# Whole casts in three PSUM slots, a four-tile output projection, border strips, two-step sums and new engine orders in a fused attention and convolution kernel

## The chip, the cores and the metric

The kernel runs on one core of a Trainium2 chip. The metric is the device time of one execution in microseconds (us); lower is better. Before the change the median of three runs is 110.3 us.

## What is computed

The input x holds 8 images of 16 x 16 tokens with 64 channels, all fp32. Four layers follow one another:

```python
# L0: self-attention over the 256 tokens of an image, 8-wide queries and keys, residual
out = softmax(relu(x@wq+bq) @ relu(x@wk+bk).T) @ (x@wv+bv) + x
# L1: group norm over pairs of channels, self-attention with 64-wide q and k, residual
h = group_norm(x); x = x + nin(softmax(q@k.T / 8) @ v, Wo, bo)
# L2: "hex" attention: each token attends to itself and 6 neighbours, 8 heads of 8
scores = einsum(qh, kh) / sqrt(8)            # 7 scores for each token and head
ctx    = einsum(softmax(scores), vh)         # neighbours outside the image: zero vectors
x = layernorm(x + ctx@out_w.T + out_b)
x = layernorm(x + relu(x@w1.T+b1)@w2.T+b2)
# L3: 1x1 conv (64 -> 128), grouped 3x3 conv, 1x1 conv (128 -> 64), with batch norms
out = relu(conv3(relu(bn(conv2(relu(bn(conv1(x))))))) + x)
```

## The kernel before

**Layout.** Channels lie on partitions. Two images make a pair (partitions 0 to 63 and 64 to 127), so there are PAIRS = 4 tiles of 128 x 256; two pairs make a group of 512 columns (GROUPS = 2). Each engine has its own instruction stream, written out by hand as a list of calls at the end of its block (`scalar`, `vector`, `tensor`, `gpsimd`), and semaphores tie them together. The four streams run in order, so the lists of calls set what stands behind a waiting instruction. PSUM has 8 banks of 512 fp32 columns, assigned by hand.

**Attention stage (L0 and L1).** There are 16 softmaxes n (8 images, two layers). For each: `scores` (TensorE, L933), `maxes` (VectorE, L663), `exps` (ScalarE, L438), `normalise` (VectorE, L668 and L672), `transposes` (TensorE, L944), `copy_probT` (ScalarE, L445). For each pair: `attend` (TensorE, L964) and `residual` (VectorE, L682). Between the layers a pair goes through `stats`, `group_variance`, a power on GpSimd (`grs`, L368) and `group_norm` (VectorE, `hT`, L702), then `project1`. In the same loop GpSimd fills `k2` and `v2`, the padded key and value tiles of the hex layer, with their bias, one half of a tile (128 x 648) per pair (L379). Only the border of them survives: `keys2` and `values2` overwrite the middle.

**Hex stage (L2).** `project2_*` makes q, k, v. VectorE forms q*k for the 7 neighbours in three runs of 3, 2 and 2 (`key_products`, L262); TensorE sums over the 8 channels of a head (`head_sums`, L1071); VectorE takes the maximum away (`shifted_scores`, L718, L719), ScalarE exponentiates, VectorE normalises (`weights`, L725 to L731; for group 1 the sum over neighbours is made by TensorE, `exp_sums`, L1080). Then `cast(j, quarters)` (L1097) spreads the weights of pair j over the channels of a head, each quarter of 64 tokens from 32 rows into a bank of its own (banks 0 to 3), and `weighted_values(j, h)` (VectorE, L741) multiplies half a pair with the neighbours' values, again in three runs. One cast of two quarters fills what one `weighted_values` empties. The seven products go to the output projection: GpSimd adds pairs of them (L405; for pairs 0 and 2 also the seventh, L409), TensorE multiplies the three sums by the 128 x 128 block-diagonal `outc` (`out_sums`, L1117), and for pairs 1 and 3 the seventh product by itself (`out_single`, L1110). `centre_input` (L1103) adds the centred residual, all into D_BANK (banks 4 and 5).

**Norms, feed-forward, convolution.** `squares` (ScalarE, L516), `variance` (TensorE, L1143), `log_variance` and `inverse_std` (ScalarE, L521, L528), `layer_norm` (VectorE, L758) for n = 0 to 3; `feed_forward1` (L1156), `relu_ff` on ScalarE (image 0 of a pair) and VectorE (image 1), `centre_normed` (L1164), `feed_forward2` (L1171). Then `conv1` (L1185), nine taps of 32 x 32 tiles in `conv2` (L1192), `conv3` (L1216), and `finish`: VectorE adds the residual (L786) and clips at zero (L787), SyncE sends three pieces of the output.

**Start.** SyncE issues the DMAs of the four pairs of x and of table `p2`; ScalarE those of `p0`, `pv`, `p1`, and then loads its function table. ScalarE waits for `consts`, the last GpSimd fill (L355), ahead of its first activation.

## Time and profile before

| | us |
|---|---|
| median of 3 runs | 110.3 (110.25 to 111.28) |
| the profiled execution | 110.36 |
| its span, first to last instruction | 108.3 |
| TensorE busy | 98.4 (91%) |
| VectorE busy | 70.6 (65%) |
| ScalarE busy | 54.2 (50%) |
| GpSimd busy | 31.8 (29%) |

PE is TensorE's matmul row and PEld its weight loads, DVE is VectorE, ACT is ScalarE, POOL is GpSimd, SP is SyncE. "L672" is a line of the kernel. Busy time of PE overlaps within a group, since its matmuls are pipelined; an fp32 matmul shows as two records, so "x4" after a matmul line can be two matmuls. Rows of one line that follow one another are merged in the timeline: start, time from the first start to the last end, engine, line, names, shape, count.

### The profile page before, as it was taken

To read this page: it belongs to the slowest core of one execution; us is meant where nothing else is said; L and a number is where in the kernel's file an instruction comes from. 1 tells how busy PE (TensorE), PEld (TensorE's weight loads), DVE (VectorE), ACT (ScalarE), POOL (GpSimd) and SP (SyncE) were. 2 spreads that over 40 slices of the span, in tenths; PEclk is the share of its full clock that TensorE was granted. 3 is DMA by queue.
4 is the path that set the end of the run, shared out by engine and by line. 5 is a ranking of instruction groups with operands and counts; after the bars stand their busy time and mean duration, and the time that the engine had idled before them with its cause. 6 is when DMAs were issued, how large, how long until landed. Compare 5 with 4: busy or idle time off the path is not lost.

```text
span 108.3 us, 2233 instructions
## 1 busy us (share of the span) xinstructions
PE 98.4 (91%) x834; PEld 51.9 (48%) x834; DVE 70.6 (65%) x166; ACT 54.2 (50%) x143; POOL 31.8 (29%) x46
## 2 busy tenths in 40 slices
PE   4978899899978999999989999999999998999960
PEld 1435768475646565453822563555322222467420
DVE  2029989989799958999999785498222522200292
ACT  2317969957989799991700400242367454200220
POOL 8960000919547910000004634962000201100000
PEclk9999999999999999999999999999999999999999
DMA  2991000000000000000000000000000000000005
GB/s 82 286 395 60 0 0 0 6 3 3 0 0 0 6 0 0 0 6 0 0 0 0 0 0 6 0 0 0 0 0 0 3 0 9 0 0 6 0 0 194
DMA packets 1594, 2.88 MB, mean 27 GB/s; under 512 B 176, under 2 KB 1200, under 8 KB 1584
## 3 DMA queue, kind: packets, MB, share of 16 engines
q1 hardware_dynamic: 1152, 2.09, 5.4%
q10 hardware_dynamic: 432, 0.67, 2.0%
q8 instruction: 6, 0.10, 0.4%
q14 instruction: 4, 0.03, 0.1%
HBM read 2.23 MB, written 0.52 MB: 25 GB/s over the span
## 4 chain that ended last, share of the span: by engine, by line
PE 54%; DVE 25%; ACT 7%; POOL 5%; issue 5%; POOLq 0%; ACTq 0%; DVEq 0%
PE quad L1097 6%; PE quad L1192 5%; PE bank L1117 4%; PE quad L933 4%; PE quad L1156 4%; DVE probn L672 4%; DVE nmax L663 3%; PE bank L1171 3%; PE bank L944 3%; ACT prob L438 3%; PE duo L1143 3%; PE bank L964 3%; PE duo L1192 3%; DVE ffh L262 2%; DVE ffh L741 2%
## 5 line engine op out<-in xcount | busy, mean ns | idle before, releaser
L438 ACT ACTIVATE prob<-quad,nmax 128x256 f32<-128x256 f32 x32 | 15.0, 483 | 2.5 <-DVE nmax L663 2.3
L944 PE MATMUL bank<-pv,probn 128*128 128x128 f32 x64 | 10.3, 283 | 1.7 <-DVE probn L672 1.1
L663 DVE TENSOR_REDUCE nmax<-quad 128x2 f32<-128x512 f32 x16 | 10.6, 682 | 1.5 <-PE quad L933 1.5
L672 DVE TENSOR_SCALAR probn<-prob,rrec 128x256 f32<-128x256 f32 x32 | 11.1, 390 | 0.6
L445 ACT ACTIVATE probT<-bank 128x512 f32<-128x512 f32 x16 | 9.6, 603 | 3.4 <-PE bank L944 3.2
L944 PEld LDWEIGHTS bank<-pv,probn 128*128 128x128 f32 x64 | 6.9, 141 | 6.1 <-DVE probn L672 3.7
L1192 PE MATMUL quad<-pads,ctaps 32*32 32x512 f32 x144 | 9.2, 595 | 0.0
L1192 PE MATMUL bank<-pads,ctaps 32*32 32x512 f32 x72 | 9.2, 596 | 0.0
L516 ACT ACTIVATE sq<-bank,prep2t 128x512 f32<-128x512 f32 x4 | 2.7, 687 | 12.3 <-PE bank L1117 9.3
L933 PE MATMUL quad<-k,q 32*128 32x256 f32 (+1 forms) x64 | 8.1, 400 | 0.9 <-ACT q L431 0.7
L1192 PE MATMUL duo<-pads,ctaps 32*32 32x512 f32 x72 | 8.8, 593 | 0.0
L964 PE MATMUL bank<-probT,v 128*64 128x256 f32 x56 | 7.6, 392 | 0.0
L1097 PE MATMUL quad<-att,head_cast 32*128 32x448 f32 x32 | 7.2, 585 | 0.4 <-DVE att L731 0.4
L368 POOL TENSOR_TENSOR grs<-gvar,minus_half 128x1 f32<-128x1 f32 x4 | 2.3, 565 | 16.8 <-DVE gvar L697 16.8
L438 ACT ACTIVATION_READ_ACCUMULATOR prob<-quad,nmax 128x1 f32 x32 | 6.9, 215 | 0.0
L933 PEld LDWEIGHTS quad<-k,q 32*128 32x128 f32 (+1 forms) x64 | 5.1, 185 | 3.2 <-ACT q L431 1.5
L416 POOL TENSOR_SCALAR x<-xhat,p,b3f 128x512 f32<-128x512 f32 x2 | 1.5, 766 | 17.1 <-DVE xhat L758 17.1
L741 DVE TENSOR_TENSOR ffh<-quad,v 128x256 f32<-128x256 f32 (+1 forms) x12 | 4.8, 462 | 2.7 <-PE quad L1097 2.7
L405 POOL TENSOR_TENSOR avsum<-qkprod 128x384 f32<-128x384 f32 x4 | 4.0, 995 | 7.4 <-DVE qkprod L741 7.4
L758 DVE SCALAR_TENSOR_TENSOR xhat<-bank,prep2t,rstd 128x512 f32<-128x512 f32 x4 | 3.0, 748 | 3.8 <-ACT rstd L528 3.7
L741 DVE TENSOR_TENSOR qkprod<-quad,v 128x256 f32<-128x256 f32 (+1 forms) x12 | 4.9, 461 | 0.6 <-PE quad L1097 0.6
L780 DVE TENSOR_SCALAR ffh<-bank,bnsh 128x256 f32<-128x256 f32 x2 | 0.9, 478 | 6.5 <-PE bank L1192 6.5
(184 smaller groups left out, 206.3 us busy)
## 6 DMA issues: line engine op xcount, KB each, us to landing
p<-in_p SPq DMA_DIRECT2D x1, 1012.5 KB, 7.0
xT<-in_xT SPq DMA_DIRECT2D x4, 128.0 KB, 4.0
p<-in_p ACTq DMA_DIRECT2D x1, 448.0 KB, 5.1
out_dram<-xT SPq DMA_DIRECT2D x1, 256.0 KB, 2.1
out_dram<-xT SPq DMA_DIRECT2D x2, 128.0 KB, 1.7
pv<-in_pv ACTq DMA_DIRECT2D x1, 128.0 KB, 3.2
p<-in_p ACTq DMA_DIRECT2D x1, 74.5 KB, 3.0
```

What stands on the lines that cost most here:

```text
L438: s.activation(prob[:, n % 3, b, :], S_BANK[n % 4][:, b * TOK:(b + 1) * TOK], ACT.Exp, bias=nmax[:, n, b:b + 1], accum_out=rsum[:, n, b:b ...
L445: s.activation(flat(probT[:, n % 4, :, :]), T_BANK, ACT.Copy).then_inc(probT_sb, 1)
L663: v.tensor_reduce(nmax[:, n, :], S_BANK[n % 4].rearrange("p (b m) -> p b m", b=BLK), AX.X, ALU.max, negate=True).then_inc(max_ready, 1)
L672: v.tensor_scalar(probn[:, n % 2, b, :], prob[:, n % 3, b, :], rrec[:, n, b:b + 1], None, ALU.mult).then_inc(norm_done, 1)
L741: ins = v.tensor_tensor(products[j][:, k0:k1, tokens], cast_half(h)[:, k0:k1, :, :], hexview(v2, j, run, SIDE // 2, SIDE // 2 * h), ALU.mult)
L933: ins = mm(S_BANK[2 * (p % 2) + i][:, b * TOK:(b + 1) * TOK], q[own, b * 128:b * 128 + 128], k[own, :], start=True, stop=True)
L944: ins = nc.tensor.transpose(T_BANK[:, mb * TOK + b * 128:mb * TOK + b * 128 + 128], probn[:, n % 2, b, mb * 128:mb * 128 + 128], ident)
L964: ins = mm(OUT_BANK[p][64 * i:64 * i + 64, 0:TOK], val[:, 2 * j + mb, 64 * i:64 * i + 64], probT[:, (2 * p + i) % 4, mb, :], start=mb == 0 ...
L1097: mm(bank[q][:, 0:NB * QTOK], head_cast[quarter_rows(q), 2 * q + jp, :], flat(att[quarter_rows(q), gr, :, :]), start=True, stop=True).then ...
L1117: ins = mm(o, outc, value_sums[j][:, k, :], start=False, stop=j % 2 == 1 and k == NB // 2 - 1)
L1156: ins = mm(bank[FH * i + h], w1g[own, 128 * h:128 * h + 128], xhat[own, gr, :], start=True, stop=True)
L1192: ins = mm(CONV2_BANKS[c][32 * q:32 * q + 32, :], ctaps[own, t, :], pads[own, c, :, ty:ty + SIDE, tx:tx + SIDE], start=t == 0, stop=t == T ...
```

## The change

Seven things change, and the mathematics stays the same.

1. **PSUM.** One tensor `psum` of 8 banks takes the place of `quad`, `low` and `duo`. `cast(j)` always casts a whole pair, all four quarters. A half pair u = 2j + h lies in slot u % 3: banks 0-1, 2-3 or 6-7. `cast(j)` waits until the half that used its second slot is multiplied.
2. **Output projection.** Odd pairs of images are swapped in the input (`x[1::2] = x[1::2, ::-1]`). `centre_input`, `out_single` and `out_sums` work on a group at a time with four 64 x 64 tiles of 256 columns, each half pair into its own partitions of two banks (4-5 for group 0, 6-7 for group 1). `layer_norm`, `squares` and `variance` of the first norm read and write these two half banks.
3. **Border strips.** GpSimd fills only the border of `k2` and `v2`: four strips, placed ahead of the loop over pairs.
4. **Sums in two steps.** GpSimd makes two of the three sums when two runs of a half are multiplied, the third after the last run; the seventh product (neighbour 2 of the first run) goes to TensorE alone for all pairs. `weighted_values` raises its semaphore after each run. `exp_sums` is gone; VectorE sums the weights for both groups.
5. **Idle matmuls.** `keep_busy()` is a 128 x 128 by 256 matmul of zeros; five of them stand around `cast(1)`.
6. **Clipping** of the output moves from VectorE to ScalarE.
7. **Orders.** The lists of calls of ScalarE, VectorE and TensorE are laid out anew; the `pv` DMA goes to SyncE's queue after the second pair of x, and `p1` is issued after the table load.

```diff
-        quad = ... [128, 4, 512]; low = ...; duo = ... [128, 1024]
+        psum = ctx.enter_context(nc.psum_tensor("psum", [128, 8, 512], F32))
+        D_IN = [psum[:, 4:6, 0:TOK], psum[:, 6:8, 0:TOK]]
+        CAST_BANK = (0, 2, 6)
...
+            for buf, k in ((k2, 1), (v2, 2)):
+                top_bottom, sides = buf[:, :, 0:PAD:PAD - 1, :], buf[:, :, 1:PAD - 1, 0:PAD:PAD - 1]
...
-                g.tensor_scalar(buf[:, 2 * h:2 * h + 2, :, :]..., zeros[:, :], col("in_proj_b", k), ...)
...
-                ins = g.tensor_tensor(total, terms[:, 0:NB - 1:2, :], terms[:, 1:NB - 1:2, :], ALU.add)
+                pool.wait_ge(avprod_sb, HALF_RUNS * m + 2)
+                g.tensor_tensor(total[:, 0:2, :], terms[:, 0:4:3, :], terms[:, 1:5:3, :], ALU.add)...
+                pool.wait_ge(avprod_sb, HALF_RUNS * m + 3)
+                g.tensor_tensor(total[:, 2, :], terms[:, 5, :], terms[:, 6, :], ALU.add)...
...
-            def cast(j, quarters=range(QUARTERS)):
+            def cast(j):
+                if j == 1:
+                    pe.wait_ge(hex_shift, GROUPS)
+                if j:
+                    pe.wait_ge(avprod_sb, HALF_RUNS * (2 * j - 1))
+                for q in range(QUARTERS):
...
+            def out_sums(gr, last):
+                j = 2 * gr
+                pe.wait_ge(avsum_sb, 4 * (j + 1) + (4 if last else 3))
+                for r in (2,) if last else (0, 1):
+                    for i in range(2):
+                        own = HALF[i]
+                        mm(D_IN[gr][own, 0, :], outc[own, own], value_sums[j][own, r, :], ...)
+                        ins = mm(D_IN[gr][HALF[1 - i], 1, :], outc[own, own], value_sums[j + 1][own, r, :], ...)
...
-                v.tensor_scalar(fin[:, columns], x3[:, columns], 0.0, None, ALU.max).then_inc(fin_sb, 1)
+                s.activation(fin[:, columns], x3[:, columns], ACT.Relu).then_inc(fin_sb, 1)
```

GpSimd, from the power of the first pair on, before: the borders (`k` and `v` from `zeros`) lie between the powers `grs` of the pairs.

```order
L361 TENSOR_SCALAR wqk1g<-p 128x256
L368 TENSOR_TENSOR grs<-gvar,minus_half 128x1
L372 TENSOR_SCALAR wvo1g<-wvo,p 128x128
L379 TENSOR_SCALAR k<-zeros,p 128x648
L368 TENSOR_TENSOR grs<-gvar,minus_half 128x1
L375 TENSOR_SCALAR ob<-wvo,gmv,p 128x1
L379 TENSOR_SCALAR k<-zeros,p 128x648
```

And after the change:

```order
L372 TENSOR_SCALAR wqk1g<-p 128x256
L379 TENSOR_SCALAR k<-zeros,p 128x4x2x18
L379 TENSOR_SCALAR k<-zeros,p 128x4x16x2
L379 TENSOR_SCALAR v<-zeros,p 128x4x2x18
L379 TENSOR_SCALAR v<-zeros,p 128x4x16x2
L385 TENSOR_TENSOR grs<-gvar,minus_half 128x1
```

Four fills of 128 x 648 inside the loop became four of 144 and 128 columns ahead of it.

TensorE in the second half of the hex stage, before (`quad` from `att,head_cast` is a cast, `bank` from `avsum`, `prob`, `qkprod` or `ffh` the projection, `duo` from `sq` the variance):

```order
L1097 MATMUL quad<-att,head_cast 128x448 x2
L1117 MATMUL bank<-avsum,prep2t 128x256 x3
L1097 MATMUL quad<-att,head_cast 128x448 x4
L1143 MATMUL duo<-sq,p 128x512
L1117 MATMUL bank<-prob,prep2t 128x256 x3
L1110 MATMUL bank<-ffh,prep2t 128x256
L1156 MATMUL quad<-xhat,w1g 128x512 x2
L1117 MATMUL bank<-prob,prep2t 128x256 x3
L1156 MATMUL quad<-xhat,w1g 128x512 x2
L1143 MATMUL duo<-sq,p 128x512
```

After the change, around the first two casts (`psum` from `zeros` is an idle matmul, from `zT` the centred residual):

```order
L1082 MATMUL psum<-ffh,p2 32x448 x4
L1103 MATMUL psum<-att,head_cast 128x448 x4
L1120 MATMUL psum<-zeros 128x256 x2
L1103 MATMUL psum<-att,head_cast 128x448 x4
L1120 MATMUL psum<-zeros 128x256 x3
L1115 MATMUL psum<-zT,p1 64x256
L1116 MATMUL psum<-zT,p1 64x256
L1115 MATMUL psum<-zT,p1 64x256
L1116 MATMUL psum<-zT,p1 64x256
L1103 MATMUL psum<-att,head_cast 128x448 x4
```

Casts come whole, the projection in rounds of four 64-row tiles behind them, and no sum stands between the two `feed_forward1` calls any more.

VectorE at the end of the hex scores, after the change (`ffh` from `q,k` is a key product, `ssum` to `att` are `weights`, `smax` and `sexp` are `shifted_scores`):

```order
L737 TENSOR_TENSOR sexp<-psum,smax 128x448
L265 TENSOR_TENSOR ffh<-q,k 128x768
L265 TENSOR_TENSOR ffh<-q,k 128x512 x2
L742 TENSOR_REDUCE ssum<-sexp 128x64
L743 RECIPROCAL srec<-ssum 128x64
L744 TENSOR_TENSOR att<-sexp,srec 128x448
L736 TENSOR_REDUCE smax<-psum 128x64
L737 TENSOR_TENSOR sexp<-psum,smax 128x448
L753 TENSOR_TENSOR qkprod<-psum,v 128x3x128
```

All key products now stand ahead of `weights(0)`, and `shifted_scores(1)` ahead of the first weighted values; before, it stood behind the first of them.

## Rows read from the trace of the kernel before

**Rows 1.** The page: busy time of each engine.

```profile
PE 98.4 (91%) x834; PEld 51.9 (48%) x834; DVE 70.6 (65%) x166; ACT 54.2 (50%) x143; POOL 31.8 (29%) x46
```

**Rows 2.** Busy by stage: start:end, length, PE, PEld, DVE, ACT, POOL, PE clock.

```profile
8.01:46.17 38.16, 35.52 (x288) 23.10 (x286) 34.38 (x97) 32.49 (x104) 13.73 (x19) 1.00 0.02 7
46.17:72.61 26.44, 26.02 (x166) 13.09 (x164) 22.41 (x45) 8.25 (x18) 9.01 (x12) 1.00 0.01 1
```

**Rows 3.** Timeline: a border fill on POOL, and VectorE with and without one.

```profile
24.96 0.41 DVE L702 TENSOR_SCALAR hT<-yT,gmv,grs 128x256 f32<-128x256 f32 x1
...
28.89 1.98 POOL L379 TENSOR_SCALAR v<-zeros,p 128x648 f32<-128x648 f32 x1
28.93 0.90 DVE L702 TENSOR_SCALAR hT<-yT,gmv,grs 128x256 f32<-128x256 f32 x1 [0.68 <-POOL grs L368]
...
29.94 1.07 DVE L672 TENSOR_SCALAR probn<-prob,rrec 128x256 f32<-128x256 f32 x2
...
45.08 0.62 DVE L672 TENSOR_SCALAR probn<-prob,rrec 128x256 f32<-128x256 f32 x2
```

**Rows 4.** Groups by line and shape, DVE, 12 to 46 us: busy, mean ns.

```profile
L672 DVE TENSOR_SCALAR probn<-prob,rrec 128x256 f32<-128x256 f32 x30 | 10.5, 393 | 0.5
...
L702 DVE TENSOR_SCALAR hT<-yT,gmv,grs 128x256 f32<-128x256 f32 x4 | 2.6, 659 | 0.7 <-POOL grs L368 0.7
```

**Rows 5.** Timeline of the hex stage, DVE.

```profile
46.17 2.98 DVE L262 TENSOR_TENSOR qkprod<-q,k 128x512 f32<-128x512 f32 x4
...
53.13 0.91 DVE L725 TENSOR_REDUCE ssum<-sexp 128x64 f32<-128x448 f32 x1
...
70.26 2.35 DVE L741 TENSOR_TENSOR ffh<-quad,v 128x384 f32<-128x384 f32 x6 [1.22 <-PE quad L1097]
```

**Rows 6.** Waits over the whole span: total us, times, longest.

```profile
DVE ffh L741 <- PE quad L1097: 2.7, 3, 1.2
```

**Rows 7.** Timeline of the hex stage, PE and POOL.

```profile
46.81 0.43 PE L1047 MATMUL quad<-zT,p 64*64 64x256 f32 x1
...
47.30 0.60 PE L1059 MATMUL quad<-zT,p 64*64 64x256 f32 x4
...
66.72 1.02 PE L1097 MATMUL quad<-att,head_cast 32*128 32x448 f32 x4
...
67.53 1.00 POOL L405 TENSOR_TENSOR prob<-ffh 128x384 f32<-128x384 f32 x1 [1.31 <-DVE ffh L741]
...
68.61 0.46 POOL L409 TENSOR_TENSOR prob<-prob,ffh 128x128 f32<-128x128 f32 x1
...
69.16 1.03 PE L1097 MATMUL quad<-att,head_cast 32*128 32x448 f32 x8
```

**Rows 8.** The first layer norm's steps: two groups of the page, one timeline row.

```profile
L516 ACT ACTIVATE sq<-bank,prep2t 128x512 f32<-128x512 f32 x4 | 2.7, 687 | 12.3 <-PE bank L1117 9.3
L758 DVE SCALAR_TENSOR_TENSOR xhat<-bank,prep2t,rstd 128x512 f32<-128x512 f32 x4 | 3.0, 748 | 3.8 <-ACT rstd L528 3.7
...
72.01 0.63 ACT L528 ACTIVATE rstd<-lnv 128x512 f32<-128x512 f32 x1
```

**Rows 9.** The chain that ended last, in order of time: start, us, what.

```profile
73.53 1.13 PE quad L1156 x4
74.65 1.49 PE bank L1117 x6
...
77.20 1.06 PE duo L1143 x2
...
79.12 1.87 PE bank L1171 x8
...
87.14 1.06 PE quad L1185 x4
```

**Rows 10.** Timeline of the end: the first residual sum, the last clipping.

```profile
103.68 0.69 DVE L786 TENSOR_TENSOR sq<-bank,x 128x512 f32<-128x512 f32 x1
...
105.86 0.29 DVE L787 TENSOR_SCALAR xT<-sq 128x256 f32<-128x256 f32 x1
```

More of the change, by code:

```diff
@@ L636, in _ @@
             conv2_out(1)
+            for n in range(len(RESULTS)):
+                finish(n)
         @block.vector
@@ L801, in _ @@
             maxes(5)
+            values0(1)
             residual(0)
@@ L1112, in out_sums @@
-            def out_sums(j):
-                o = D_BANK[j // 2][:, TOK * (j % 2):TOK * (j % 2) + TOK]
-                pe.wait_ge(avsum_sb, 2 * j + 2)
-                for k in range(NB // 2):
-                    ins = mm(o, outc, value_sums[j][:, k, :], start=False,
-                             stop=j % 2 == 1 and k == NB // 2 - 1)
-                ins.then_inc(av_used, 1)
+                if gr == 0:
+                    pe.wait_ge(k2_sb, PAIRS)
+                    pe.wait_ge(v2_sb, PAIRS)
+                else:
+                    pe.wait_ge(avprod_sb, HALF_RUNS * (2 * (PAIRS - 1)))
@@ new lines, in out_sums @@
+            def out_sums(gr, last):
+                j = 2 * gr
+                pe.wait_ge(avsum_sb, 4 * (j + 1) + (4 if last else 3))
+                for r in (2,) if last else (0, 1):
+                    for i in range(2):
+                        own = HALF[i]
+                        mm(D_IN[gr][own, 0, :], outc[own, own], value_sums[j][own, r, :], start=False, stop=last)
+                        ins = mm(D_IN[gr][HALF[1 - i], 1, :], outc[own, own], value_sums[j + 1][own, r, :],
+                                 start=False, stop=last)
+                if last:
+                    ins.then_inc(av_used, 1)
```

343 lines of the change are left out of this document (172 added, 171 removed).

## The prediction

> **What bounds the kernel now.** Start with the page's busy line [rows 1]. TensorE is busy for 91% of the span and VectorE for 65%, which looks like a TensorE kernel. The busy times by stage say otherwise for the first two thirds [rows 2]. From 8.0 to 46.2 us (attention), VectorE works 34.4 of 38.2 us, ScalarE 32.5 and TensorE 35.5; matmuls are pipelined, so TensorE's number is partly waiting inside a row. From 46.2 to 72.6 us (hex stage) VectorE works 22.4 of 26.4 us, ScalarE only 8.3. TensorE shows 26.0 there. Read the waits to see who holds whom: the rows that wait in that stage are VectorE's for casts [rows 6], 2.7 us in three waits, and the last of them, 1.22 us, stands before the last two halves [rows 5]. So VectorE and TensorE alternate in the hex stage. Behind it the chain of waits is TensorE all the way to conv1 [rows 9].
>
> I measure everything from two marks: X, the start of the row at 46.17 (key products, behind the last `normalise` but one residual) [rows 5], and C, the start of conv1 at 87.1 [rows 9]. Before X the two kernels do the same VectorE work in another order; behind C the order is unchanged up to conv3.
>
> **Part 1, attention up to X: 2.0 us earlier.** Look at `hT` with and without a fill of GpSimd beside it [rows 3]: 0.41 us alone, 0.90 us beside the fill at 28.89. Two `probn` take 0.62 us alone and 1.07 us beside it. The group rows [rows 4] sum this up. `hT` means 659 ns over 4: 4 x (0.66 - 0.41) = 1.0 us too long. `probn` means 393 ns over 30; one of an undisturbed pair is about 0.35 us (a pair of two overlapping rows takes 0.62), so 30 x 0.04 = 1.3 us. In all the four fills cost VectorE 2.3 us, on the engine that is busy 90% of this stage. The change moves the fill ahead of the loop and shrinks it: 144 + 128 + 144 + 128 columns. By the row of 648 columns (1.98 us, about 3 ns a column) and that of 128 columns two inputs wide (0.46 us) [rows 3, 7] a strip costs 0.4 to 0.65 us, some 2.5 us in all between about 8 and 11 us, when VectorE mostly waits and takes maxima. GpSimd's next duty is the first pair's power, near 18 us, so nobody waits for them. The strips have inner runs of two elements, which no row shows; between 0.4 us each and three times that (as if each element cost three times a column) they still end before 16 us.
>
> The Trainium skill (page "SBUF — State Buffer", section "Who interferes with whom") says that VectorE in its two-port mode and GpSimd lock a shared pair of ports, and that the loser blocks for the whole other instruction. The trace agrees on who disturbs whom but not on the size: `hT` starts at 28.93 and ends at 29.83, while the fill ends at 30.87 [rows 3]. By the page `hT` would end after 30.87, and removing the fills would give up to 4 x 2 us; by the rows it is 2.3 us.
>
> How much of 2.3 us reaches X? I walked the new order on all four engines with the durations of the rows. VectorE keeps idle gaps: before, 38.2 - 34.4 = 3.8 us of gaps and handovers [rows 2]; my walk (order by order, no wait skipped) has about 0.3 us more, since maxima stand earlier and `normalise` later. It reaches X at about 44.2: 2.0 us earlier. The bounds: nothing, if another engine (ScalarE 32.5, TensorE 35.5 of 38.2) takes over as the limit; 3.3 us, if the new order also fills a third of the gaps. A negative bound is 0.5 us, if a maximum placed early waits for its scores as often as before and in a worse place. I take 2.0.
>
> The start gives nothing: ScalarE's first activation waits for GpSimd's `consts`, and this is unchanged. The earlier warm-up matmul and the moved `pv` and `p1` DMAs are hidden by it; `p1` lands perhaps 1 us later and is first needed by GpSimd's weight fill, whose user comes at 18 us or later.
>
> **Part 2, X to C: 2.2 us shorter** (40.9 us before). First VectorE from X on. Before, the last half ended at X+26.4, and 22.4 us of that was work [rows 2]: 2.7 us went to the three casts of [rows 6] and 1.0 us to a wait for the first cast of pair 1 and one for `exp_sums`, the rest to handovers. Without these waits and with the 0.91 us of summing that `weights(1)` now does itself [rows 5], the last half ends at 26.4 - 3.7 + 0.9 = X+23.7. Counted back in halves of 1.2 us (2.35 for two) [rows 5], half (2,0) ends at X+20.1, and half (1,1) at X+18.9; `weights(1)` ends at X+17.3.
>
> Are the casts in time? A whole cast of four quarters takes 1.03 us and one of two quarters 1.02 [rows 7]: seven casts become four, 3 us less for TensorE, and `exp_sums` goes too. The five idle matmuls (0.5 us each, a third of the 1.49 of [rows 9]) stand where TensorE waits for the first half and for `weights(1)`, and are hidden there. `cast(1)` waits for the first half (X+13.2) and ends as VectorE comes for it. `cast(2)` follows `weights(1)` and is ready at X+18.4, before X+18.9. `cast(3)` needs the slot of half (2,0) and stands behind `out_sums(0)`, which waits for GpSimd's first step of half (1,1) (X+19.4): it runs from X+20.5 to 21.5, and VectorE waits 0.2 us. The last half ends at X+23.9 and not at X+26.4.
>
> What is late next is the first norm. Behind `cast(3)`: a last round of the sums 0.5, `squares` 0.69, `variance` 1.06 [rows 9], logarithm 0.69 (as `squares`), exponential 0.63, `layer_norm(0)` 0.75 [rows 8] and 0.4 for handovers: it ends at X+26.2. I add 0.2 us for changes between whole and four-tile matmuls, which no row prices. `feed_forward1` then starts at X+26.5 and not at X+27.4 (73.53) [rows 9]: 0.9 of the 2.5 us are left.
>
> The projection: a round of four 64 x 64 tiles of 256 columns is 47.30 - 46.81 = 0.49 us [rows 7], as much as one full matmul of 256 columns (a third of 1.49) [rows 9]. Per group 4 rounds take the place of 7 matmuls, 2.0 for 3.5 us, and in the second group they end at about X+26, beside the norm. So the 1.49 us of sums between the two `feed_forward1` [rows 9] leaves the chain. From there TensorE is back to back: `feed_forward1`, `variance`, `feed_forward1`, `centre_normed` at 1.06 each (the last taken as the others), `feed_forward2` at 1.87 [rows 9], and the same again: 12.2 us, so C is X+38.7 and was X+40.9.
>
> GpSimd's sums in two steps have 256 and 128 columns, by interpolation between 1.00 (384) and 0.46 us (128) [rows 7] 0.73 + 0.46, with handovers 1.3 us for a half that VectorE makes in 1.2. It falls behind by some 0.4 us over five halves: the steps of the last half are ready at about X+24.6 and 25.1, as TensorE's rounds want them. Were GpSimd to lag 1 us more, C would be up to 0.6 us later.
>
> ScalarE's new order puts `relu_ff(0, 0)` behind the second logarithm, 1.5 us later than it could be. TensorE has `feed_forward1(0, 1)` and `centre_normed(0)` to do meanwhile; the cover is 0.7 us, and when it is gone each tenth costs a tenth. Bounds of part 2: 0.7 us shorter (the norm's gain is eaten, of the sums' 1.49 half remains) to 3.0 us (no handover costs anything).
>
> **Part 3, the end: 0.2 us.** Adding and clipping alternate on VectorE from 103.68 to 106.15 [rows 10]. With clipping on ScalarE the three sums end at about 105.1, and the last clippings take between 0.29 us (as on VectorE) [rows 10] and 0.69 (ScalarE, 512 columns) [rows 8] each; with a handover the last ends at about 105.95. Bounds: 0 to 0.5 us.
>
> **Sum.** The profiled execution took 110.36 us, 2.1 us beyond its span of 108.3 and 0.06 above the median. 110.36 - 2.0 - 2.2 - 0.2 = 106.0.
>
> **Rivals.**
> - *Attention gives back what the fills free.* ScalarE gets a denser order and VectorE's gaps grow from 3.8 to 6 us: X stays, and the time is 106.0 + 2.0 = 108.0. For it: TensorE and ScalarE are nearly as busy as VectorE there [rows 2]. Against it: they run a chain around VectorE's steps, and those get shorter.
> - *More gain.* The new order also fills a third of the gaps: 106.0 - 1.3 = 104.7. For it: the gaps exist. Against: I could not find it in the walk.
> - *Cancelled, within 1%.* No gain at X, and the first norm late enough (GpSimd behind by 1.5 us, `relu_ff` uncovered) that C gains 0.7 only: 110.36 - 0.7 - 0.2 = 109.5. It needs two unlikely things together.
> - *Slower: the four tiles run one after the other.* Two of them write one bank from different row halves. If the four took turns, a round would cost 4 x 0.49, 1.5 us more; behind `cast(3)` there are six rounds (sums, centre, four of group 1), 9 us, of which 1 us is covered: 106.0 + 8 = 114.0. It makes the change slower from about 0.9 us a round on. The Trainium skill (page "TensorEngine Tiling (Array Packing)", section "Gotcha 1: PSUM Pressure") says that different row tiles cannot access the same bank at once, which speaks for this. Against it: L1047 and L1049 each write one bank from both row halves too, and their round takes 0.49 us [rows 7]. So for this form the trace disagrees with the rule.
>
> **Chances.** Forecast, 105.1 to 107.1: 0.57. Attention gives back (107.1 to 109.2): 0.21. More gain (below 105.1): 0.12. Cancelled: 0.05. Slower: 0.05. The range from 104.4 to 108.2 takes in the forecast, half of the first rival and most of the second. A measurement of this kernel can tell about 1% from no change. Faster by over 1% (below 109.2): 0.90; within 1%: 0.05; slower: 0.05.
>
> **What would show it.** Right, step by step: `hT` at 0.41 us four times and `probn` mean near 350 ns; the first key products behind the last `normalise` near 42.2 and the mark X near 44.2; VectorE's eight halves ending 23.9 us behind X with one wait for a cast; a projection round at 0.5 us; no sums between the `feed_forward1` calls; conv1 near 82.9; TensorE's clock at 1.0 throughout. Wrong: X later than 45.7, VectorE waiting over 1 us for casts, a round over 0.7 us, or TensorE waiting for `relu_ff(0, 0)`.

## The result, and the profile of the changed kernel

The changed kernel takes 107.88 us (median of 4 executions, 107.12 to 109.63); the kernel before, run beside it, 110.78 us (median of 4). The ratio is 0.972, with a 95% interval from 0.964 to 0.980. The forecast was 106.0 us with a range from 104.4 to 108.2. The profiled execution took 107.2 us with a span of 105.3, so it is 3.16 us below the profiled execution of before (110.36). Executions more than 1.5% above the fastest one of the same kernel are left out of every ratio in this document but not out of the medians, so a ratio can differ from the quotient of two medians.

The page of the changed kernel, span and busy line, answers to [rows 1]:

```profile
span 105.3 us, 2327 instructions
...
PE 93.4 (89%) x882; PEld 48.9 (46%) x882; DVE 68.4 (65%) x165; ACT 54.9 (52%) x146; POOL 26.3 (25%) x50
```

TensorE has 48 more matmul records and is busy for 5.0 us less. GpSimd is busy for 5.5 us less. VectorE's share is still 65%. As before, the line doesn't say where the time went; the marks of the prediction do. X is the first row of the last key products on VectorE, C the first matmul of conv1.

The groups of VectorE from 12 to 46 us answer to [rows 4] (busy us, mean ns, idle before):

```profile
L690 DVE TENSOR_SCALAR probn<-prob,rrec 128x256 f32<-128x256 f32 x30 | 9.2, 350 | 0.6
...
L720 DVE TENSOR_SCALAR hT<-yT,gmv,grs 128x256 f32<-128x256 f32 x4 | 1.7, 416 | 0.2
```

`hT` fell from 659 to 416 ns and `probn` from 393 to 350. By these means that frees 2.3 us of VectorE's time, as worked out.

The timeline of VectorE in the hex stage answers to [rows 5] and [rows 6]:

```profile
45.40 2.98 DVE L265 TENSOR_TENSOR qkprod<-q,k 128x512 f32<-128x512 f32 x4
...
67.22 2.34 DVE L753 TENSOR_TENSOR ffh<-psum,v 128x384 f32<-128x384 f32 x6 [0.22 <-PE psum L1103]
```

One wait for a cast is left, 0.22 us long, where three took 2.7 us. The last half ends at 69.56, X + 24.2.

The chain that ended last, from the first norm to conv1, answers to [rows 9]:

```profile
71.96 1.13 PE psum L1183 x4
73.09 1.06 PE psum L1165 x4
...
75.21 1.05 PE psum L1191 x2
76.26 1.87 PE psum L1198 x8
...
84.23 1.06 PE psum L1212 x4
```

L1183 is `feed_forward1`. Before, 1.49 us of sums stood behind the first one; now `variance` (1.06) stands there, and TensorE is back to back.

The balance of the two profiled executions, by marks:

| Stretch | before, us | after, us | difference | predicted |
|---|---|---|---|---|
| span's start to the first maxima | 8.01 | 8.83 | +0.82 | 0 |
| first maxima to X | 38.16 | 36.57 | -1.59 | -2.0 |
| X to C | 40.90 | 38.76 | -2.14 | -2.2 |
| C to the first residual sum | 16.61 | 16.60 | 0.0 | 0 |
| first residual sum to the end | 4.62 | 4.54 | -0.1 | -0.2 |

C is the start of conv1 in the timeline, 87.07 before and 84.16 after; the chains have 87.14 and 84.23. The sum is -3.0 us of span. So the middle went almost as forecast, and the one stretch that the prediction called unchanged, the start, became longer. This is its timeline:

```profile
1.15 1.28 ACT L433 ACT_TABLE_LOAD   x1 [1.15 <-PEq L1438]
1.18 0.42 ACTq L434 DMA_DIRECT2D p<-in_p  x1
1.62 0.42 SPq L347 DMA_DIRECT2D pv<-in_pv  x1
2.09 0.91 SPq L345 DMA_DIRECT2D xT<-in_xT  x2
3.97 2.97 PE L913 MATMUL psum<-xT,p 128*64 128x256 f32 x8 [0.86 <-DMA p<-in_p]
7.04 0.47 ACT L441 ACTIVATE q<-psum,p 128x256 f32<-128x256 f32 x1 [2.89 <-PE psum L913]
7.70 1.26 PE L944 MATMUL psum<-k,q 32*128 32x256 f32 x16 [0.76 <-DVE k L672]
```

ScalarE's table load runs from 1.15 to 2.43 us, and its DMA for `p1` goes out at 1.18 all the same. The change was written with the DMA behind the table load, and I had it land 1 us later; it goes out 0.46 us earlier than before (1.64), and its 448 KB are under way with the input. The first projection then ends at 6.94 us. It ended at 6.13 before.

### The profile page after: what moved, and what is told of

It is laid out like the page before. It is cut to its first block, busy times and chain, and to the rows that moved or that the text cites. A ratio compares the mean times of both kernels' runs of the same rounds, so it can differ in the third digit from the quotient of the medians.

```text
span 105.3 us, 2327 instructions
## 1 busy us (share of the span) xinstructions
PE 93.4 (89%) x882; PEld 48.9 (46%) x882; DVE 68.4 (65%) x165; ACT 54.9 (52%) x146; POOL 26.3 (25%) x50
## 4 chain that ended last, share of the span: by engine, by line
PE 55%; DVE 18%; ACT 15%; issue 5%; DMA 3%; POOL 1%; ACTq 0%; DVEq 0%
PE psum L1219 10%; ACT prob L448 6%; PE psum L955 4%; PE psum L944 4%; PE psum L1183 4%; PE psum L1103 4%; PE psum L1198 4%; DMA p<-in_p 3%; PE psum L975 3%; DVE nmax L681 3%; PE psum L913 3%; PE psum L1139 3%; DVE probn L690 2%; DVE qkprod L753 2%; PE psum L1165 2%
## 5 line engine op out<-in xcount | busy, mean ns | idle before, releaser
L448 ACT ACTIVATE prob<-psum,nmax 128x256 f32<-128x256 f32 x32 | 14.9, 481 | 2.2 <-DVE nmax L681 2.0
L1219 PE MATMUL psum<-pads,ctaps 32*32 32x512 f32 x288 | 12.0, 594 | 0.0
L681 DVE TENSOR_REDUCE nmax<-psum 128x2 f32<-128x512 f32 x16 | 10.6, 680 | 2.1 <-PE psum L944 2.1
L455 ACT ACTIVATE probT<-psum 128x512 f32<-128x512 f32 x16 | 9.7, 605 | 1.8 <-PE psum L955 1.4
L955 PE MATMUL psum<-pv,probn 128*128 128x128 f32 x64 | 10.4, 285 | 0.1
L944 PE MATMUL psum<-k,q 32*128 32x256 f32 (+1 forms) x64 | 8.1, 399 | 1.2 <-DVE k L672 0.8
L1219 PEld LDWEIGHTS psum<-pads,ctaps 32*32 32x32 f32 x288 | 6.6, 103 | 5.1 <-issue 2.2
L955 PEld LDWEIGHTS psum<-pv,probn 128*128 128x128 f32 x64 | 6.9, 144 | 4.3 <-issue 3.7
L975 PE MATMUL psum<-probT,v 128*64 128x256 f32 x64 | 8.7, 392 | 0.1
L448 ACT ACTIVATION_READ_ACCUMULATOR prob<-psum,nmax 128x1 f32 x32 | 6.8, 213 | 0.0
```

Source lines behind the costliest of these rows:

```text
L448: s.activation(prob[:, n % 3, b, :], S_BANK[n % 4][:, b * TOK:(b + 1) * TOK], ACT.Exp, bias=nmax[:, n, b:b + 1], accum_out=rsum[:, n, b:b ...
L455: s.activation(flat(probT[:, n % 4, :, :]), T_BANK, ACT.Copy).then_inc(probT_sb, 1)
L681: v.tensor_reduce(nmax[:, n, :], S_BANK[n % 4].rearrange("p (b m) -> p b m", b=BLK), AX.X, ALU.max, negate=True).then_inc(max_ready, 1)
L944: ins = mm(S_BANK[2 * (p % 2) + i][:, b * TOK:(b + 1) * TOK], q[own, b * 128:b * 128 + 128], k[own, :], start=True, stop=True)
L955: ins = nc.tensor.transpose(T_BANK[:, mb * TOK + b * 128:mb * TOK + b * 128 + 128], probn[:, n % 2, b, mb * 128:mb * 128 + 128], ident)
L975: ins = mm(OUT_BANK[p][64 * i:64 * i + 64, 0:TOK], val[:, 2 * j + mb, 64 * i:64 * i + 64], probT[:, (2 * p + i) % 4, mb, :], start=mb == 0 ...
```

## The experiments

All timed runs had the kernel before beside them on the same chip; a ratio below is to that. The profiles of different kernels are compared mark by mark, since executions of one kernel here differ by 1 to 2 us (why is told under "What was not expected"). The number of executions is given with each median. "The changed kernel" is the one of the result.

### The input DMAs

**The order of before.** The changed kernel with its input DMAs as they were:

```diff
-            act.dma_start(packed["p0"][:, :], t["p0"]).then_inc(tables_in["p0"], 16)
+            for p in ("p0", "pv", "p1"):
+                act.dma_start(packed[p][:, :], t[p]).then_inc(tables_in[p], 16)
             s.preload_act_table_set("natural_log_exp_and_others")
-            act.dma_start(packed["p1"][:, :], t["p1"]).then_inc(tables_in["p1"], 16)
```

(and `pv` is taken out of SyncE's queue.)

> The changed kernel with the input DMAs issued as before the change (ScalarE: p0, pv, p1, then the table load; SyncE: the four pairs of x, then p2). Theory A: the changed kernel starts late because p1 (448 KB) is now issued at 1.18 us, ahead of pv, and takes bandwidth from the second pair of x; its first project0 ends at 6.94 us instead of 6.13. Then here it ends near 6.1, the first queries0 starts near 6.3 (GpSimd's consts), and the kernel is 0.8 us faster than the changed one (profiled near 106.4). Theory B: the late start is chance of that execution, or something else in the start (the smaller warm-up fill): first queries0 stays near 7.0 and the time near 107.2.

Measured: 108.26 us (6 executions), ratio 0.963 (0.955 to 0.972). The projection ends at 6.19 us and the queries start at 6.30, 0.74 us earlier than in the changed kernel:

```profile
6.30 0.47 ACT L439 ACTIVATE q<-psum,p 128x256 f32<-128x256 f32 x1 [2.26 <-POOL head_cast L364]
...
6.95 2.20 PE L942 MATMUL psum<-k,q 32*128 32x256 f32 x16 [0.75 <-DVE k L670]
```

The 0.8 us at the start are the DMA order's. The smaller fill and the earlier warm-up matmul of the changed kernel are in this one too, so they aren't the cause. But the second row spoils the comparison: the same 16 matmul records took 1.26 us in the changed kernel and take 2.20 here, so the first maxima come at 9.03 all the same. A gain in the time isn't shown either: the ratio rests on two of the six executions and its interval overlaps that of the changed kernel (0.964 to 0.980); by the medians of all executions it is 108.26 to 111.23, or 0.973.

**`p1` behind the second input part.** SyncE issues x0, x1, `p1`, x2, x3, `p2`; ScalarE `p0`, `pv` and then loads its table.

```diff
                 if j == 1:
-                    sp.dma_start(packed["pv"][:, :], t["pv"]).then_inc(tables_in["pv"], 16)
+                    sp.dma_start(packed["p1"][:, :], t["p1"]).then_inc(tables_in["p1"], 16)
```

> The changed kernel with p1 issued on SyncE's queue behind the second pair of x, and pv behind p0 on ScalarE's. Theory A (p1 competes with the second pair of x): project0 ends at about 5.2 to 5.8 us, earlier than in either kernel, but ScalarE's first activation still waits for consts at 6.25, so the time is that of e1, near 106.4. If the second pair of x sets the start by its own place in the queue and not by p1, project0 ends as in e1, near 6.1. Theory B (chance): near 7.0 and 107.2. A rival loss: p1 or the third and fourth pairs land too late for prepare and project0(1) (needed near 9 to 10 us), which would show as a TensorE wait for a DMA.

Measured: 107.31 us (6 executions: 107.74, 106.32, 108.76, 106.5, 106.87, 108.29), ratio 0.959 (0.954 to 0.964). The projection ends at 6.11 us and the scores again take 2.20. `p1` goes out at 1.63 and does no harm there. All the profiles agree on this. In the seven kernels that issue `p1` at 1.18 or 1.19 us (the changed one and six runs below) the projection ends at 6.72 to 7.05 us. In the four that issue `pv` at about 1.15 and `p1` at 1.62 or 1.63 (this run, the one before it and the two with small matmuls below) it ends at 6.06 to 6.19. `pv` and `p1` moved together in all of them, so which of the two moves costs the 0.8 us is read from the sizes (128 and 448 KB) and not shown by itself. The three lowest executions are within 0.9 us of the 106.0 forecast.

### The border strips

**Whole fills again** in the changed kernel, in the loop as before, each padding two images:

```diff
-            for buf, k in ((k2, 1), (v2, 2)):
...
+            borders = [(buf, k, h) for buf, k in ((k2, 1), (v2, 2)) for h in range(GROUPS)]
...
+                g.tensor_scalar(buf[:, 2 * h:2 * h + 2, :, :].rearrange("p a b c -> p (a b c)"),
+                                zeros[:, :], col("in_proj_b", k), None, ALU.add).then_inc(kv2_border, 1)
```

> The changed kernel with GpSimd's four fills of 128 x 648 back in the loop over pairs in place of the strips. Theory A: VectorE's hT and probn beside a fill are stretched again, 2.3 us in all, and most of it reaches the end: 1.5 to 2.3 us slower than the changed kernel (109.0 near). Theory B: the new order of attention has made ScalarE and TensorE the limit there, so VectorE's stretch is covered: under 0.8 us slower.

Measured: 109.37 us (6 executions), ratio 0.982 (0.976 to 0.987), an interval that overlaps that of the changed kernel, so the time doesn't decide between the two theories, and the marks below don't either. VectorE's groups show the fills back, a little smaller than in before:

```profile
L689 DVE TENSOR_SCALAR probn<-prob,rrec 128x256 f32<-128x256 f32 x31 | 10.1, 367 | 0.6
...
L719 DVE TENSOR_SCALAR hT<-yT,gmv,grs 128x256 f32<-128x256 f32 x4 | 2.5, 630 | 0.3
```

`hT` gets 4 x 0.21 = 0.9 us longer and `probn` 31 x 0.017 = 0.5 us: 1.4 us on VectorE. From the first maxima to X it takes 37.86 us. The kernels with the same slow first scores take 36.9 to 38.2 without the fills, so this run alone does not size what arrives at X.

**Strips alone**, in the kernel before:

```diff
...
+            for buf, k in ((k2, 1), (v2, 2)):
+                top_bottom, sides = buf[:, :, 0:PAD:PAD - 1, :], buf[:, :, 1:PAD - 1, 0:PAD:PAD - 1]
+                for strip, shape in ((top_bottom, (PAIRS, 2, PAD)), (sides, (PAIRS, SIDE, 2))):
+                    n = shape[0] * shape[1] * shape[2]
+                    g.tensor_scalar(strip, zeros[:, 0:n].rearrange("p (a b c) -> p a b c", a=shape[0], b=shape[1]),
+                                    col("in_proj_b", k), None, ALU.add).then_inc(kv2_border, 1)
...
-                g.tensor_scalar(buf[:, 2 * h:2 * h + 2, :, :].rearrange("p a b c -> p (a b c)"),
-                                zeros[:, :], col("in_proj_b", k), None, ALU.add).then_inc(kv2_border, 1)
```

> The kernel before with only GpSimd's fills replaced by the four strips ahead of the loop. Theory A: the strips alone bring the gain of attention: mark X (key products) moves from 46.2 to about 44.5, total 1.5 to 2.0 us faster than before (about 108.6). Theory B: it is the new order that turns VectorE's freed time into an earlier end; under the old order the freed time turns into waits and X moves by less than 0.8 us.

Measured: 109.96 us (6 executions), ratio 0.987 (0.982 to 0.992). Here the first scores take 1.26 us, as in before, and the marks can be compared. From the first maxima to X it takes 36.98 us, 1.18 less than before; from X to C 40.90, the same.

```profile
L673 DVE TENSOR_SCALAR probn<-prob,rrec 128x256 f32<-128x256 f32 x30 | 9.3, 351 | 0.5
...
L703 DVE TENSOR_SCALAR hT<-yT,gmv,grs 128x256 f32<-128x256 f32 x4 | 1.6, 407 | 0.7 <-POOL grs L373 0.7
```

The fills cost 10.5 + 2.6 - 9.3 - 1.6 = 2.2 us of VectorE's time in before, and 1.2 us of it arrives at X, between what the two theories had. The 0.7 us that `hT` waits for GpSimd's `grs` in the last row were there before as well [rows 4] and hold none of the rest. What grew is the maxima's wait for their scores, first before, then here:

```profile
L663 DVE TENSOR_REDUCE nmax<-quad 128x2 f32<-128x512 f32 x12 | 8.0, 682 | 0.2 <-PE quad L933 0.2
...
L664 DVE TENSOR_REDUCE nmax<-quad 128x2 f32<-128x512 f32 x12 | 8.1, 685 | 1.0 <-PE quad L934 1.0
```

Freed of the fills, VectorE comes to its maxima before TensorE has the scores, and 0.8 us of the freed time turn into that wait. The new order of the changed kernel takes another 36.98 - 36.57 = 0.4 us from this stretch.

### The hex stage

**Two slots for the casts** instead of three:

```diff
-        CAST_BANK = (0, 2, 6)
+        CAST_BANK = (0, 2)
...
-                    pe.wait_ge(avprod_sb, HALF_RUNS * (2 * j - 1))
+                    pe.wait_ge(avprod_sb, HALF_RUNS * (2 * j))
```

(and the bank is chosen by the remainder of 2.)

> The changed kernel with whole casts in two slots (banks 0-1 and 2-3) in place of three: each cast waits until both halves of the pair before are multiplied. Theory A (the third slot is what lets whole casts hide): VectorE waits about 1.1 us for each of casts 1, 2 and 3, so the last half ends 2 to 3 us later behind mark X, and conv1 1.5 to 3 us later. Theory B (weights(1) and GpSimd's sums set the pace): only one wait appears, under 1 us, and conv1 moves by less than 0.7 us.

Measured: 112.71 us (10 executions), ratio 1.004 (0.997 to 1.011). The whole gain of the change is gone. X to C is 42.0 us, 3.25 more than with three slots:

```profile
62.54 0.89 DVE L753 TENSOR_TENSOR qkprod<-psum,v 128x384 f32<-128x384 f32 x2 [1.21 <-PE psum L1103]
...
68.19 2.35 DVE L753 TENSOR_TENSOR ffh<-psum,v 128x384 f32<-128x384 f32 x6 [1.21 <-PE psum L1103]
71.75 2.35 DVE L753 TENSOR_TENSOR ffh<-psum,v 128x384 f32<-128x384 f32 x6 [1.21 <-PE psum L1103]
```

A whole cast with two slots can't start before both halves of the last one are read, so VectorE waits for it in full: 1.21 us, three times, 3.6 us. Whole casts pay only with the third slot. Five of the ten executions took 113.4 to 114.5 us with a mean granted clock of 0.966 to 0.985, the others 110.3 to 112.1 us with 1.00, so with two slots the clock also falls in part of the executions; the profile shown is one with 1.00.

**No idle matmuls.** The five calls of `keep_busy` are left out of the changed kernel; they compute nothing that is used.

```diff
             cast(0)
-            keep_busy()
-            keep_busy()
             cast(1)
-            keep_busy()
-            keep_busy()
-            keep_busy()
             centre_input(0)
```

> The changed kernel without its five idle matmuls. Theory A: nothing depends on them: from mark X to conv1 still 38.8 us, matmul rows behind them unchanged (a whole cast 1.03 us), same time. Theory B: without them TensorE is idle for some 2 us twice, and its clock falls from the 2.4 to the 1.2 GHz level in the stage behind: the rows of casts and sums double (cast 2 us) and conv1 comes 2 us or more later.

Measured: 112.1 us (10 executions), ratio 1.000 (0.994 to 1.005); the ratio rests on three of the ten, and the median of before beside them is 111.0. Theory A expected next to nothing and fell. All ten executions had a mean granted clock of 0.946 to 0.969, so the profiled one (0.947) shows what happens in each. The page's slices of the granted clock, and the windows around them (start:end, length, PE, PEld, DVE, ACT, POOL, clock):

```profile
PEclk9999999999999999999999555599999999999997
```

```profile
58.00:60.00 2.00, 1.08 (x12) 0.34 (x8) 1.92 (x4) 0.00 (x0) 0.00 (x0) 1.00 0.00 0
60.00:62.00 2.00, 0.63 (x4) 0.55 (x8) 2.00 (x6) 0.58 (x1) 1.03 (x2) 0.82 0.00 0
62.00:64.00 2.00, 2.00 (x16) 0.30 (x8) 1.07 (x4) 0.00 (x0) 1.23 (x3) 0.50 0.00 0
64.00:66.00 2.00, 0.31 (x4) 0.00 (x0) 1.93 (x4) 0.00 (x0) 0.72 (x1) 0.50 0.00 0
66.00:68.00 2.00, 1.28 (x8) 0.55 (x8) 1.70 (x5) 0.00 (x0) 1.01 (x2) 0.50 0.00 0
68.00:70.00 2.00, 2.00 (x20) 0.93 (x20) 1.37 (x4) 0.00 (x0) 0.99 (x3) 0.50 0.04 8
70.00:72.00 2.00, 2.00 (x24) 0.75 (x16) 0.97 (x3) 0.00 (x0) 1.86 (x4) 0.62 0.00 0
```

TensorE works 1.08 and then 0.63 of 2 us, and in the second of these windows the granted clock falls from 1.00 to 0.50, the level of 1.2 GHz. It stays there until about 71 us. The casts take 1.03 us before and 1.88 after:

```profile
58.94 1.03 PE L1103 MATMUL psum<-att,head_cast 32*128 32x448 f32 x8 [0.89 <-DVE att L744]
...
66.72 1.88 PE L1103 MATMUL psum<-att,head_cast 32*128 32x448 f32 x8 [2.41 <-DVE qkprod L753]
```

X to C is 41.7 us, 2.9 more. The kernel before had no idle matmuls and a clock of 1.00 there [rows 2]: its seven casts, `exp_sums` and sums kept TensorE busier. With whole casts and fewer matmuls the clock falls in this stage, and with the five idle matmuls it doesn't.

**Group 0's last sums ahead of `cast(3)`:**

```diff
             out_sums(0, False)
-            cast(3)
             out_sums(0, True)
+            cast(3)
```

> The changed kernel with the last sums of group 0 ahead of cast(3) in TensorE's order. In the changed kernel squares(0) waits for them until 67.8 us, and the first layer norm (71.1) is what feed_forward1 (71.96) waits for. Theory A (the chain from cast(3) over the first norm sets conv1): squares(0) starts about 1.0 us earlier, cast(3) and the last two halves 0.4 us later, and conv1 0.4 to 0.8 us earlier behind mark X (38.8 us now). Theory B (the last sums of group 1, which need the last half, set it): feed_forward1 does not move, or moves 0.4 us later with the halves.

Measured: 108.81 us (4 executions), ratio 0.981 (0.976 to 0.987). Group 0's squares start at X + 21.3, 1.1 us earlier, and VectorE waits 0.65 us for the last cast instead of 0.22. X to C stays at 38.79 us. The chain has moved:

```profile
69.88 0.73 POOL prob L418
70.61 0.41 POOL prob L420
71.02 0.72 POOL prob L418
...
73.31 1.06 PE psum L1183 x4
```

Now the last half's sums on GpSimd and group 1's rounds hold TensorE's order. So two chains of nearly the same length end at `feed_forward1`: the norm of group 0, and the sums of group 1. Shortening one of them gives nothing, as theory B had it: `feed_forward1` starts at X + 26.7 and not at X + 26.6.

**`relu_ff(0, 0)` ahead of the second logarithm:**

```diff
             squares(1)
-            log_variance(1)
             relu_ff(0, 0)
+            log_variance(1)
```

> The changed kernel with relu_ff(0, 0) of ScalarE ahead of the second logarithm. Theory A (the prediction's): TensorE has feed_forward1(0, 1) and centre_normed(0) to do until then, so the place of relu_ff(0, 0) is covered: from mark X to conv1 still 38.8 us. Theory B: feed_forward2(0, 0) waits for it: conv1 0.3 us or more earlier behind X.

Measured: 108.9 us (4 executions), ratio 0.978 (0.974 to 0.983). `relu_ff(0, 0)` runs at X + 27.8 instead of X + 29.4, and X to C is 38.73 (38.76). The cover that the prediction saw is there.

### The end

**Clipping on VectorE**, as in before:

```diff
-                v.tensor_tensor(x3[:, columns], b, x2.rearrange("p g n -> p (g n)")[:, columns], ALU.add)\
-                    .then_inc(x3_sb, 1)
+                done(v.tensor_tensor(x3[:, columns], b, x2.rearrange("p g n -> p (g n)")[:, columns], ALU.add))
+                v.tensor_scalar(fin[:, columns], x3[:, columns], 0.0, None, ALU.max).then_inc(fin_sb, 1)
```

(and ScalarE's `finish` calls are left out.)

> The changed kernel with clipping on VectorE again, as before the change. Theory A (the prediction's): from the first residual sum to the last clipping 2.47 us as before the change, against 1.97 now, and the end of the span 0.1 to 0.3 us later, since the output's DMAs are issued one behind the other anyway. Theory B: the last DMA sets the end, and the end of the span behind the first residual sum stays 4.5 us.

Measured: 108.97 us (4 executions), ratio 0.980 (0.975 to 0.984). First the changed kernel's end, then this one's:

```profile
100.76 1.35 DVE L797 TENSOR_TENSOR sq<-psum,x 128x512 f32<-128x512 f32 x3
101.49 1.24 ACT L558 ACTIVATE xT<-sq 128x512 f32<-128x512 f32 x3 [0.91 <-DVE sq L797]
102.14 1.32 SPq L351 DMA_DIRECT2D out_dram<-xT  x3
```

```profile
102.92 0.69 DVE L795 TENSOR_TENSOR sq<-psum,x 128x512 f32<-128x512 f32 x1
...
104.10 1.65 SPq L351 DMA_DIRECT2D out_dram<-xT  x3
...
105.10 0.29 DVE L796 TENSOR_SCALAR xT<-sq 128x256 f32<-128x256 f32 x1
```

The last clipping ends 1.97 us behind the first sum's start with ScalarE and 2.47 with VectorE. But from the first sum to the span's end it is 4.54 and 4.6 us: 0.5 us on the engines give at most 0.1. The first output part leaves 1.38 us behind the first sum's start with ScalarE's clipping and 1.18 with VectorE's, SyncE issues three parts one behind the other, and the third is issued by 2.70 and by 2.83 us: of the 0.5 us on the engines 0.13 are left when the last part goes out.

### TensorE's first microseconds

The slow first scores (2.20 us for 16 records against 1.26) appeared in so many kernels that they needed runs of their own. Theory A: what TensorE does in its first microseconds decides. All three start from the kernel with `p1` behind the second input part.

**Small matmuls in the gaps.** One matmul of zeros with 128 columns stands behind the warm-up, and one behind the first projection:

```diff
             keep_warm(bank[0], WARM_UP)
+            mm(bank[0][:, 0:128], zeros[:, 0:128], zeros[:, 0:128], start=True, stop=True)
...
             project0(0)
+            mm(bank[0][:, 0:128], zeros[:, 0:128], zeros[:, 0:128], start=True, stop=True)
             scores(0)
```

> The kernel of e2 with one 128-column matmul of zeros behind the warm-up matmul and one behind the first project0. In executions of one kernel the first scores take 1.26 us or 2.20 us: TensorE's rows change from the 1.2 to the 2.4 GHz level either before 6.9 us (before, changed, e4) or only between 10.7 and 12.9 us (e1, e2, e3), and times of one kernel differ by 1 to 2 us. Theory A: idle time of TensorE in the first 7 us decides which; with the two gaps filled most executions are in the early group, and of six times at most one lies 1 us above the lowest. Theory B: it is a matter of when the execution starts against something free-running: the mix stays near half and half.

Measured: 106.44 us (6 executions: 106.34, 106.33, 107.76, 106.49, 107.61, 106.39), ratio 0.963 (0.957 to 0.969). Four of six are below 107 us, where the kernel without them had three. Theory A expected at most one of six to lie 1 us above the lowest, and two do; that doesn't tell the theories apart. The profile happens to be one with fast first scores:

```profile
6.81 1.27 PE L945 MATMUL psum<-k,q 32*128 32x256 f32 x16 [0.34 <-ACT q L441]
```

It is the run that shows what the prediction's other steps make when the start is as assumed: first maxima at 7.97 (8.01 before), X at 44.52 (predicted 44.2), C at 83.28, total 106.34 (predicted 106.0).

**No warm-up matmul at all:**

```diff
             pe.wait_ge(warm_ready, 1)
-            keep_warm(bank[0], WARM_UP)
```

> The kernel of e2 without the warm-up matmul of zeros: TensorE's first work is project0 near 3.8 us. Theory A (work in the first microseconds decides when TensorE's rows change to the 2.4 GHz level): none of six executions has fast rows before 6.9 us; the profiled one has the first scores at 2.20 us, and all times lie in the upper group, 107.4 us and more. Theory B (nothing TensorE does there matters, only when the execution starts): still about half of the times near 106.3.

Measured: 108.71 us (6 executions, 107.44 to 109.22), ratio 0.973 (0.969 to 0.978), against 0.959 (0.954 to 0.964) with it. No execution is below 107 us. The profile has the slow scores:

```profile
7.11 2.20 PE L943 MATMUL psum<-k,q 32*128 32x256 f32 x16 [0.75 <-DVE k L672]
```

So TensorE's work before the first projection matters, as theory A says and as far as six executions can show it; that the gaps behind it do is not shown.

**The wait for `consts` moved** behind ScalarE's first exponentials, added to the kernel with the small matmuls:

```diff
-            act.wait_ge(consts, 1)
             queries0(0)
...
             exps(3)
+            act.wait_ge(consts, 1)
             prepared_act()
```

> The kernel of e8 (p1 behind the second pair of x, two small idle matmuls in the gaps of the start) with ScalarE's wait for consts moved from its first activation to behind exps(3). Theory A: the start is bound by the first project0 (ends near 6.1 us) and by consts (6.25 us) alike; only their difference is to be had: the first queries0 starts at 6.1 to 6.2 and not 6.3, and the lowest time is 106.2 to 106.3 us (e8: 106.33). Theory B: consts was the limit of the start and the matmuls before it only look slow: the first scores start 0.4 us earlier or more, lowest time under 106.0.

Measured: 106.25 us (6 executions: 105.59, 105.82, 106.07, 106.44, 106.81, 107.56), ratio 0.954 (0.950 to 0.957). `queries0` starts at 6.13 and waits for the projection, no longer for GpSimd:

```profile
6.13 0.47 ACT L441 ACTIVATE q<-psum,p 128x256 f32<-128x256 f32 x1 [2.20 <-PE psum L914]
```

The queries start 0.15 us earlier, as theory A had it, but the lowest time, 105.59 us, is 0.74 below that of the kernel with the small matmuls, and under the 106.0 of theory B. The scores start at 6.85 us, no earlier than there (6.81), so theory B's reason doesn't show in this profile either, and where the 0.74 us come from is open. The profile is of the slowest execution (107.56 us) and has slow first scores (2.21 us), although both small matmuls are there: filling the gaps doesn't make scores of 1.26 us certain. This is the best version found. Its interval lies wholly below that of the changed kernel (0.964 to 0.980) and touches that of the kernel with the small matmuls alone (0.957 to 0.969).

## Why the prediction was right, and where it missed

The forecast was 1.9 us too low against the median and 1.2 against the profiled execution; the result is inside the range and the sign is right. That the median lies inside took luck as well. Three of the kernels above (group 0's sums first, `relu_ff(0, 0)` first, clipping on VectorE) have the changed kernel's input DMAs and, by their marks from X on, cost 0.1 us more or less at most. Their medians are 108.8 to 109.0 us, above the 108.2 where the range ends, and none of their twelve executions is below 108.3, where two of the changed kernel's four are at 107.1 and 107.2. By its steps:

- **"The start gives nothing": wrong.** It was the only term of size that failed: +0.82 us in the profiled execution. I read the code as an order in time (table load, then DMA) and priced the moved `p1` as 1 us late. The trace has it 0.46 us early, ahead of `pv` and beside the input, and the projection ends 0.8 us later. The first two runs with another DMA order have the projection back at 6.11 and 6.19 us. The prediction named `consts` as the cover; it covers only what ends before 6.3 us, and the projection already ended at 6.13.
- **"Part 1: 2.0 us": right in kind, a little too much.** The rows got as short as forecast (`hT` 416 ns, `probn` 350 ns). At X 1.59 us arrive: 1.2 for the strips (shown by the strips alone) and 0.4 for the new order (the difference to it). The rival in which attention gives all of it back is out. The 0.3 us of gaps that my walk added were right: before had 38.16 - 34.38 = 3.8 us without VectorE [rows 2], and the changed kernel has 4.1 of 36.57 us. What was put too high is the work: VectorE's busy time in the stretch fell by 34.38 - 32.46 = 1.9 us and not by 2.3, and 1.9 - 0.3 is what arrives. The 2.3 us were added up from mean times of rows that partly overlap (two `probn` take 0.62 us, not 2 x 0.35); that this makes up the 0.4 us isn't shown.

```profile
8.83:45.40 36.57, 34.76 (x284) 22.68 (x282) 32.46 (x96) 31.92 (x103) 7.23 (x17) 1.00 0.01 2
```

- **"Part 2: 2.2 us": right, 2.14.** The last half ends at X + 24.2 (23.9), with one wait of 0.22 us (0.2); `layer_norm(0)` starts at X + 25.7 and `feed_forward1` at X + 26.6 (26.5). No sums stand between the `feed_forward1` calls. Of the 2.14 us, 27.36 - 26.56 = 0.8 are gained up to the first `feed_forward1` and the other 1.3 behind it; no run has the whole casts without the four-tile projection or the other way round, so this division is read from the trace alone. With two slots the gain turns into a loss of 1.0 us (42.0 for 40.9), so the third slot is worth 3.25 us by itself.
- **"The idle matmuls are hidden there": true of their time, but the step is mis-sized.** Read as a cost, they are nothing. Without them X to C takes 2.9 us more. The prediction asked for a clock of 1.0 as a sign and never priced what would hold it there. Had the change come without them, I would have forecast 106 all the same and been 6 us off, 4 more than now.
- **"A round of four tiles 0.49": right.** The rival of serial tiles is out. (Its bound in the prediction, slower "from about 0.9 us a round on", is by its own sum 0.9 us more a round: 110.4 - 106.0 + 1 us of cover, over six rounds, so a round of 1.4.)

```profile
65.10 0.43 PE L1139 MATMUL psum<-avsum,prep2t 64*64 64x256 f32 x1
...
65.12 0.43 PE L1140 MATMUL psum<-avsum,prep2t 64*64 64x256 f32 x1
65.36 0.38 PE L1139 MATMUL psum<-avsum,prep2t 64*64 64x256 f32 x1
```

  The four first passes start within 0.02 us of one another, the second passes follow at 65.36, and the four rounds of group 1 start at 69.62, 70.10, 70.57 and 71.00 us. The Trainium skill (page "TensorEngine Tiling (Array Packing)", section "Gotcha 1: PSUM Pressure") says that row tiles cannot access one bank at once; here tiles of both row halves write one bank side by side, and the trace again disagrees.
- **"GpSimd's sums 0.73 + 0.46": right,** and they are nearer to the path than the text had them: with group 0's sums moved forward they set the end.

```profile
65.62 0.73 POOL L418 TENSOR_TENSOR prob<-ffh 128x256 f32<-128x256 f32 x1 [0.16 <-DVE ffh L753]
66.30 0.46 POOL L420 TENSOR_TENSOR prob<-ffh 128x128 f32<-128x128 f32 x1
```

- **"`relu_ff(0, 0)` is covered": right,** shown by the run that has it 1.6 us earlier for no gain.
- **"Part 3: 0.2 us": 0.1,** within its bounds. The engines end 0.5 us sooner and the span keeps a fifth of that.
- **The strips' own cost**, put at 0.4 to 0.65 us, is at the upper end, and hidden as said (two of the four; the other two take 1.29):

```profile
7.17 1.32 POOL L379 TENSOR_SCALAR k<-zeros,p 128x144 f32<-128x144 f32 x2
```

The profiled execution misses 106.0 by 1.2 us: the start 0.82, attention 0.41 and the rest 0.2 short, less 0.2 because the part beyond the span was 1.9 us and not 2.1. The median lies another 0.7 us higher; part of the executions come out 1 to 2 us longer than others, in either kernel, and the next section tells what goes with that.

## What to carry to other kernels

- A moved DMA issue has to be followed to the moment when it goes out and to what then shares the lines with it; a place behind another instruction in the code is not a place behind it in time when the queue doesn't wait for that instruction.
- When a change makes TensorE's work shorter, look at where its gaps become long: the clock can fall, and matmuls of zeros in those gaps can be worth more than the work that was saved. Price both, with and without them.
- Time freed on the busiest engine arrives only in part (here half of the strips' 2.2 us), and behind an improved chain there may stand a second one of the same length: look for it before shortening the first again.

## What was not expected of the hardware

**TensorE's rows in the first microseconds take twice as long, and the moment at which this ends varies.** The warm-up matmul with 512 columns takes 2.07 us for its two passes; `centre_normed` (L1191), which has two passes of the same shape, takes 1.05 in the chain above. The first scores, 16 records, take 1.26 us in the profiles of before, of the changed kernel, of the strips alone and of the first run with small matmuls, and 2.20 us in all the others. The granted clock of the page is 1.00 in these windows in both cases, so it doesn't show the cause. The profiles with slow scores have their first maxima 0.7 to 1.2 us later than the profile with scores of 1.26 us and the same input DMAs, and without the fills they lose 0.3 to 1.6 us more before X (first maxima to X 36.9 to 38.2 us against 36.6). From X to C all kernels with the changed kernel's hex stage take 38.7 to 38.8 us, so these profiles differ in what lies before X. The kernel before spreads alike: of 23 executions beside one batch, 10 took up to 110.63 us and the others 111.0 or more; it has no profile with slow scores, so that the cause is the same there is not shown. What decides between early and late is open, beyond that without a warm-up matmul no execution had the short time of an early one.

**The clock falls in gaps of the hex stage that look short.** In the kernel without idle matmuls it left 1.00 during 60 to 62 us, after TensorE had been busy for 1.08 of 2 us and 0.63 of 2 us. It was back at 1.00 from 72 us, after windows with 2.00, 0.31, 1.28, 2.00 and 2.00 us of work (62 to 72 us). In the changed kernel no window of the hex stage shows less than 1.00, one with 0.61 of 2 us of work (62 to 64) among them, which has full windows on both sides.

**ScalarE's table load doesn't hold its DMA queue** (issue at 1.18 us, load from 1.15 to 2.43), shown in the profile of the changed kernel and in those of all runs with its input DMAs (issue at 1.18 or 1.19 us).
